# Output phase of a convolutional LSTM, attention and recurrence kernel: moments moved on TensorE, merge and reciprocals moved on VectorE

## The reference, cut to what matters

```python
sim1 = einsum(q, k_l)                   # tokens x 64 landmarks, for each of 8 heads
attn1 = softmax(sim1, axis=-1)          # row maxima, exp, sums, reciprocals of the sums
out = attn1 @ attn2_inv @ (attn3 @ v)   # attn2_inv @ (attn3 @ v) is ready: the "context"
out = out + conv(v)                     # a 33-tap convolution along the tokens
out = out @ w_out + b_out
t = t + (x + out)                       # the residual
# of the next layer: layer norm of t, then Wx = t @ W.T with batch statistics of Wx
```

## Time and profile before

| | us |
|---|---|
| median of 3 runs | 5909.51 (5907.49 to 5918.73) |
| profiled execution | 5913.64 |
| its span, first to last instruction | 5911.8 |
| reciprocals of the output phase, first to last | 2542.9 to 3575.9 |
| TensorE, VectorE, ScalarE, GpSimd busy over the span | 5253.6, 3071.2, 3138.0, 1523.0 |

### The profile page before, as it was taken

How to read it: one execution, slowest core, us unless ns; L and a number is a source line. 1 busy time by engine, 2 the same in 40 slices (tenths; PEclk the granted TensorE clock), 3 DMA queues, 4 the chain that set the end, 5 groups by cost and what they waited for, 6 DMA issues and landing times. The chain is left out here.

```text
span 5911.8 us, 223297 instructions
## 1 busy us (share of the span) xinstructions
PE 5253.6 (89%) x97395; PEld 3278.2 (55%) x97488; DVE 3071.2 (52%) x8152; ACT 3138.0 (53%) x9108; POOL 1523.0 (26%) x1905
## 2 busy tenths in 40 slices
PE   5599999997899998799999997888888888888888
PEld 4599888896566666744444444333333333333333
DVE  8677777775788886568888883111111111111111
ACT  6465555565677776378888883333333333333333
POOL 2100000002888874256666662000000000000000
PEclk7899999999999999999999998999999999999999
DMA  9631111225777773467777762111111111111100
GB/s 389 270 115 58 58 58 60 84 77 183 245 245 243 231 243 105 102 175 203 202 203 202 204 173 66 33 34 32 32 34 33 32 32 35 32 32 32 35 18 24
DMA packets 773031, 689.32 MB, mean 117 GB/s; under 512 B 67056, under 2 KB 663024, under 8 KB 767984
## 3 DMA queue, kind: packets, MB, share of 16 engines
q1 hardware_dynamic: 754672, 575.39, 32.6%
q0 software_dynamic: 14672, 95.16, 4.0%
q10 hardware_dynamic: 2736, 4.89, 0.2%
HBM read 392.17 MB, written 274.89 MB: 113 GB/s over the span
## 5 line engine op out<-in xcount | busy, mean ns | idle before, releaser
L2797 ACT ACTIVATE f_y<-f_acc 128x16 f32<-128x16 f32 x4096 | 754.7, 184 | 1542.5 <-PE f_acc L2739 1542.5
L2739 PEld LDWEIGHTS f_acc<-f_y,f_vT 128*32 128x32 f32 x32768 | 645.2, 108 | 1438.7 <-ACT f_y L2797 1437.0
L2739 PE MATMUL f_acc<-f_y,f_vT 128*32 128x16 f32 x32768 | 1046.1, 193 | 279.6 <-issue 1.5
L2697 PE MATMUL f_junk<-f_idle 128*32 128x512 bf16 x8400 | 832.5, 376 | 0.0
L2579 DVE COPY f_zT<-f_zt 128x512 f32<-128x512 f32 x124 | 85.8, 692 | 1138.4 <-PE f_zt L2653 1138.4
L2355 DVE TENSOR_REDUCE o_m<-o_bank_l 128x8 bf16<-128x512 f32 x512 | 329.7, 686 | 132.4 <-PE o_bank_l L2152 130.0
L2572 DVE TENSOR_SCALAR f_wxn<-f_wxp,f_scale,f_shift 128x512 f32<-128x512 f32 x126 | 102.1, 811 | 509.0 <-PE f_wxp L2667 508.9
L1299 ACT ACTIVATE a_p<-a_s 128x512 f32<-128x512 f32 x502 | 259.3, 602 | 153.0 <-PE a_s L1166 151.2
L2318 ACT ACTIVATE o_p<-o_bank_s 128x512 f32<-128x512 f32 x512 | 264.4, 602 | 142.0 <-PE o_bank_s L2175 142.0
L533 POOL DMA_DIRECT2D hidden<-l_h x46 | 34.7, 756 | 1162.1 <-DVE l_hsum L790 961.6
L712 ACT ACTIVATE l_gate<-l_pf,r_ctx 128x256 f32<-128x256 f32 (+7 forms) x512 | 202.5, 446 | 229.1 <-PE l_pf L643 228.8
(11 more groups left out here) (323 smaller groups left out, 11517.6 us busy)
## 6 DMA issues: line engine op xcount, KB each, us to landing
o_v<-vals SPq DMA_DIRECT2D x256, 272.0 KB, 3.4
a_hid<-hidden SPq DMA_DIRECT2D x112, 520.0 KB, 5.0
hidden<-l_h POOLq DMA_DIRECT2D x46, 1040.0 KB, 6.6
l_x<-skew SPq DMA_DIRECT2D x46, 1024.0 KB, 5.2
vals<-a_v SPq DMA_DIRECT2D x128, 272.0 KB, 3.4
gn_x<-in_x SPq DMA_DIRECT2D x16, 2048.0 KB, 17.4
a_xin<-in_x SPq DMA_DIRECT2D x128, 256.0 KB, 5.1
tokens<-a_t SPq DMA_DIRECT2D x128, 256.0 KB, 3.4
```

The source lines that it names most:

```text
L2697: nc.tensor.matmul(junk[rows, :], idle[:, 0:QUAD], idle[:, :], start=True, stop=True)
L2739: mm = nc.tensor.matmul(acc[k % 2][rows, t, :], vT[:, rows], before, start=False, stop=True, skip_group_check=True)
L2797: nc.scalar.activation(y[q][:, step, :], acc[step // RC % 2][:, step % RC, :], ACT.Sigmoid).then_inc(s_y, 1)
```

## The change

On TensorE `moments` of c-4 moves from the end of the slot to between `project` and the second call of `row_maxima`. On VectorE `reciprocals` of c-1 moves from behind `residual` to between the two pairs of `maxima`, and `merge` of c-1 from the end of the slot to ahead of `normalise` of c-2. In the tail behind the last slot `merge` and `reciprocals` of the last chunk change places. What is computed, the buffers, the DMAs and SP's order stay the same.

```diff
                     row_maxima(b, c + 1, 0, nq)
                 if precedes(c, 3, first):
                     project(b, c - 3)
+                if precedes(c, 4, first):
+                    moments(b, c - 4)
                 if follows(c, 1, last):
                     row_maxima(b, c + 1, 1, nq)
                 weigh(b, c, q)
...
                 if precedes(c, 2, first):
                     turn_convolved(b, c - 2, q if c >= 2 else 1 - q)
-                if precedes(c, 4, first):
-                    moments(b, c - 4)
...
             def slot(b, c, q, first, last):
                 if follows(c, 1, last):
-                    for k in range(GT):
+                    for k in range(2):
+                        maxima(b, c + 1, k)
+                if precedes(c, 1, first):
+                    reciprocals(b, c - 1)
+                if follows(c, 1, last):
+                    for k in range(2, GT):
                         maxima(b, c + 1, k)
                 if precedes(c, 3, first):
                     residual(b, c - 3)
                 if precedes(c, 1, first):
-                    reciprocals(b, c - 1)
+                    merge(b, c - 1)
                 if precedes(c, 2, first):
                     normalise(b, c - 2)
                     add_convolved(b, c - 2)
-                if precedes(c, 1, first):
-                    merge(b, c - 1)
...
             residual(B - 1, NG - 3)
+            merge(B - 1, NG - 1)
             reciprocals(B - 1, NG - 1)
-            merge(B - 1, NG - 1)
             normalise(B - 1, NG - 2)
```

## The result

The changed kernel takes 6136.01 us (median of 4, 6128.27 to 6139.83) against 5909.58 (median of 4): 1.038 times as long, 95% interval 1.0367 to 1.0393. The profiled execution took 6139.67 us, its span is 6137.9. Of the 226 us between the two spans 222 lie in the output phase: from the first to the last of the 128 reciprocals it was 1033.0 us, now it is 3802.4 - 2547.4 = 1255.0. The other 4.5 us lie ahead of it, where nothing was changed.

A forecast was written before the change was run, and what follows sets the result against it. The prediction took the ring through SP and VectorE, nearly level with TensorE, to bound the slot: 2.65 + 7.55 = 10.2 us. That adds 227 + 19 = 246 us, giving 6155 us, range 6085 to 6235.

The forecast's parts named there:

- What bounds the kernel: Output phase before the change: TensorE's 8.07 us a slot and the ring's 7.88 us turn are nearly level.
- the ring: Loop through VectorE and SP, once a slot: reciprocals, spread, broadcast, pack of the next chunk, next reciprocals; 7.88 us before.
- The link: Time from reciprocal to spread: grows from 0.38 to 2.65 us, through second maxima, residual and base load.
- S: Time from first spread's issue to the reciprocal that waited for the pack: stays, taken as 7.55 us (7.1 to 8.1).
- The sum: Slot period 2.65 + 7.55 = 10.2 us; 227 us over 113 turns plus 19 over 11: +246 us.
- The last 11 turns: Turns without loads of the next images' v: period 9.25 us instead of 7.51, adding 19 us.
- The count: Residual is in the ring from slot 3 to 126: 124 turns, 113 with v loads and 11 without.
- Moments: TensorE: the move gains 0.52 us of stalls, loses about 0.15, net 0.37 a slot; the wait for u is covered.
- Merge: VectorE: merge ahead of normalise costs nothing; bounds of 0 and 0.75 us only where VectorE is the bound.
- TensorE as the bound: Rival: pack always landed in time, only TensorE's 0.37 us a slot count, 5864 us; needs S under 5.05; chance 0.05.
- A pack as fast as the spread: Rival: pack takes 2.1 us instead of 3.44, period 8.8 us, about 5992 us in all; chance 0.06.
- The clock: Rival: idle TensorE gets a lower clock in the output phase, about 6465 us if in half the slots; chance 0.03.

The follow-up runs named there:

- e2: The kernel before with only moments moved, to between project and the second row maxima: 5899.5 us.
- e4: The changed kernel with load_base moved on SP's queue from ahead of spread to behind pack: 5914 us, ratio 1.0013.
- e6: The changed kernel with the residual moved on VectorE from behind the second pair of maxima to directly behind the reciprocals: 5999.6 us.
- e1: The kernel before with only the reciprocals moved, to between the two pairs of maxima: 6132.1 us.
- e3: The kernel before with only merge moved, ahead of normalise: 5913.2 us, ratio 1.001.
- f1: The kernel before with moments moved as in the change and the v loads moved to the head of SP's slot: slower by 3%.
- f3: The kernel before with only the v loads moved, to the head of SP's slot: slower by 3%.
- g3: The kernel before with moments moved as in the change and the v loads issued by ScalarE instead of SP: 6068.3 us.
- e5: The changed kernel with load_base moved one place on SP's queue, from ahead of spread to behind it: 6092.7 us.
- e7: The kernel before with moments moved as in the change and pack ahead of broadcast on SP's queue: 5924.9 us.
- e8: The changed kernel with load_base moved behind broadcast and pack, and pack ahead of broadcast, on SP's queue: 5990.9 us.

## Why the prediction was right

Forecast 6155, measured 6136; the range was 6085 to 6235. By its steps:

- *What bounds the kernel.* TensorE and the ring nearly level: e2 fits that. Of the 0.37 us a slot forecast for TensorE (0.32 by its waits) the period shows 0.16 and the medians, at 8 us over 124 slots, 0.07, which isn't clear of noise.
- *The link.* Forecast 2.65 us, measured 2.58; before it was 0.38. The parts are in the rows above: 0.27 to the maxima, 1.14 to the residual, 0.68, 0.03, then base load and spread. e4 removed it by SP's order, e6 shortened it by VectorE's.
- *S.* Forecast 7.55, measured 7.38, and in the kernel before 7.80. The mean from spread to broadcast did not change, 2.66 against 2.68: long `v` issues are fewer now, but the common value rose from 2.40 (the median before) to 2.62. That is the extra landing time behind the base load that I had bounded at 0 to 0.6 us and taken at nothing. It did no harm by luck: the one turn that I read S from had 2.72 there. The 0.4 us that S lost lie behind the pack's issue, 3.35 against 3.74: by the semaphores' times the pack lands 0.2 us sooner, and VectorE starts directly at the landing, where it came 0.2 us late on average before.
- *The sum.* S was 0.17 us too large and the link 0.07; over 113 turns that is 19 and 8 us too much.
- *The last 11 turns.* Forecast 9.25, measured 9.46, 2 us too little in all.
- *The count.* 124 turns; 124 reciprocals wait. 113 x 1.78 + 11 x 1.89 = 222 us, which is the 1255.0 - 1033.0 of the phase. The forecast had 246 for it; the medians differ by 226.
- *Moments.* The gain of 0.52 us less 0.15: the cover lost is 0.20. That `u` is ready in time was wrong in the changed kernel: 55 of 100 slots wait 0.4 us for it, since the residual is later too. It cost no time that shows: e1, without the moments' move, is as slow, since TensorE waits anyway.
- *Merge.* Costed at nothing; e3 agrees within 0.2%.
- *The rivals.* TensorE as the bound: ruled out by an S of 7.38 where under 5.05 was needed. A pack as fast as the spread: 3.35 us from its issue against 2.1; the broadcast in front of it stayed. The 2.0 us of the Trainium skill's page "DMA: Bandwidth & Descriptors", section "Anatomy of one DMA", would have given S of 5.9 and the mean was 7.38. That section's table is for DMAs that GpSimd issues, and SP issues these; for the spread the trace agrees all the same, 2.06 us from its second issue to the broadcast. The runs with bulk in front of the spread (f1, f3, g3) show how far a measurement may be from that fixed cost: 3.6 to 3.8 us. The clock: 0.98 from 2600 to 3490 us, where TensorE was busy 720 of 890 us, so it had its 2.4 GHz nearly all the time.

What I got wrong stands in the experiments: four times I took S for a property of the DMAs and moved bulk loads about it (e5, f1, f3, g3), and each time S grew by 1.3 to 1.9 us. Three more kernels that should have won (e4, e7, e8) uncovered a wait next to the one that was removed.

## What to carry to other kernels

Where several engines and a DMA queue pass something round once per iteration, add up the turn of that ring and set it beside the busiest engine: here they were 7.9 and 8.1 us, and the fullest engine looked like the bound. An instruction moved to be "ready earlier" brought nothing here, as its input comes from the ring. What now stands behind it enters the ring when a queue waits for it ahead of the ring's next step: the residual did, by way of the base load (e1), and ceased to when SP's order was changed (e4). What a small DMA takes to land depends on the bulk issued just ahead of it, so its time should be measured with that bulk where it will stand; of the orders tried here none was clearly faster than the first.

## What the runs showed of the hardware

- The spread, a pair of 8 KB DMAs, was followed by its waiter 2.4 us after the first issue in more than half of the turns of the kernel before, 2.6 with a 256 KB load directly in front (changed), 4.9 to 5.1 with 1312 KB issued in the 2.6 us before (f3, f1), and 4.4 with 768 KB of these on the same queue and the 544 KB of `v` issued by ScalarE (g3). Another issuing engine didn't isolate it.
- The pack, 8 KB behind a 256 KB broadcast, took 2.8 us from its second issue to the reciprocal with no bulk between spread and broadcast, 3.35 with 544 KB, 4.6 with 800 KB before it (f3, changed, e5).
- TensorE busy 720 of 890 us in a regular rhythm, with waits of up to 2.4 us, was granted 0.98, the full clock but for short single stretches at half of it; busy 46 of 90 us in the group norm stage it had 0.73, by turns the full clock and half of it.
